# One change to an attention and recurrence kernel: first loads and products in another order, the image's values in a column group per head, the last projection begun on half its input with two steps held for it, and the last store on SyncE

## The chip, the cores and the metric

The kernel runs on one core of one Trainium2 chip. The metric is the device time of one execution in microseconds (us). The engines are TensorE (PE; its weight loads are PEld), VectorE (DVE), ScalarE (ACT), GpSimd (POOL) and SyncE (SP), which here only issues DMA transfers.

## The reference

Two layers with residual connections follow each other, all in float32:

```
q, k, v = split(x @ c_attn_w + c_attn_b)          # x: 8 x 512 x 512; 16 heads of 32
k = concat([cond @ uk_w.T + uk_b, k])             # one image key per sequence
v = concat([cond @ uv_w.T + uv_b, v])             # one image value per sequence
scores = where(key <= query + 1, q k' / sqrt(32), -10000) + [0, mask]
x = x + (softmax(scores) @ v) @ c_proj_w + c_proj_b
xw = x @ Wx + b                                   # for all 512 steps
h_t = tanh(h_{t-1} @ Wh + xw_t)                   # h_0 = cond
out = x + h
```

## The kernel before, in words

The 8 sequences of 512 positions are cut into 8 parts of 64 positions and two sets of four sequences: 16 trips (`TRIPS`), each of 4 sequences by 64 positions. A trip has 32 units (`UNITS`): a unit `u` is one head for two of its sequences. For each trip TensorE makes `q` and `k` in four chunks (`q`, `k`, `imgscore` for the image key), `v` in two halves (`vfirst`, `v`), for each unit `score`, `turn` (probabilities transposed), for every four units `pv`, for every 16 units `imgturn`, `rowturn` and `norm` (the image's part added to `pv`), and at the end the output projection `proj` in four chunks. Matrices that need accuracy are split into a high and a low part and multiplied in three products (lines 502 to 504). Keys and values go through DRAM (`k_dram`, `v_dram`): a store from POOL or SyncE, then loads by SyncE into `kt` and `vbuf`.

The recurrence has 512 steps. A step is 16 matmuls that each write one 32-row column group (line 1056), a transpose on DVE (line 882) and a tanh on ScalarE (line 735). 448 steps (`FIRST`) are laid between the attention work of trips 2 to 15, the last 64 follow behind the last projection. Each group of 16 steps (`out`) is transposed on TensorE, copied on ScalarE to `outs` (line 725) and stored by POOL (line 640).

What sets the order is the list that `main_order()` writes out: a pass over all units with a side list of dense work (projections of the next trip), and events without cost such as loads. `order()` places the steps in it (the `while` loop) and gives each engine its own list, sorted by the clock of TensorE's work plus a lag for each kind (`LAGS`). Every engine works its list strictly in order.

Ahead of the lists each engine has a fixed prologue. SyncE loads `ident`, `cond`, `uk_w`, four of the eight pieces of `w_qkv`, the `x` of trip 0, the other four pieces, `uv_w` and `w_proj`. TensorE transposes `cond` and `uk_w` (line 901), multiplies them (line 906, for the image key `kimg`), transposes `uv_w` (line 912, into the four `scores` banks, which ScalarE copies to `wh`, line 662), and begins with `q` of chunk 0. The product for the image value (`vimg`, line 946) comes behind chunk 0. ScalarE casts the pieces of `w_qkv` to their high part (line 651), four before and four after it casts the `x` of trip 0; DVE makes the low parts (lines 746 and 766). `wx` and `wh` hold these early matrices until POOL loads `w_x` and `w_h` into them (line 622). `wproj` on ScalarE and DVE (lines 697, 792) splits `w_proj`. ScalarE's `xsplit` (line 676) casts the `x` of the next trip, loaded by SyncE in `load_x` (line 527).

`norm` on TensorE is line 1021: for each of the four chunks one matmul of 32 rows (two sequences' 16 image probabilities) by 128 columns, into all 128 rows of `pv`. DVE then scales (`x1T`, line 860), ScalarE casts it (`attnT_hi`, line 715), DVE makes `attnT_lo` in two halves (line 865), each counted in `attn_split`; `proj` waits for all of them before its first matmul.

## Time and profile before

| | |
|---|---|
| median of 3 runs | 1640.55 us (1639.9 to 1641.07) |
| the profiled execution | 1643.75 us, of which the profile's span is 1642.0 us |
| TensorE busy | 1532.6 us (93%), 32749 matmul passes |
| DVE, ScalarE, POOL busy | 778.3, 665.1, 186.5 us |
| mean granted TensorE clock | 0.987 of full speed |
| chain that ended last | PE 86%, DVE 4%, issue 4%, ACT 4% |

### The profile page before, as it was taken

To read this page: it belongs to the slowest core of one execution; us is meant where nothing else is said; L and a number is where in the kernel's file an instruction comes from. 1 tells how busy PE (TensorE), PEld (TensorE's weight loads), DVE (VectorE), ACT (ScalarE), POOL (GpSimd) and SP (SyncE) were. 2 spreads that over 40 slices of the span, in tenths; PEclk is the share of its full clock that TensorE was granted. 3 is DMA by queue.
4 is the path that set the end of the run, shared out by engine and by line. 5 is a ranking of instruction groups with operands and counts; after the bars stand their busy time and mean duration, and the time that the engine had idled before them with its cause. 6 is when DMAs were issued, how large, how long until landed. Compare 5 with 4: busy or idle time off the path is not lost.

```text
span 1642.0 us, 74143 instructions
## 1 busy us (share of the span) xinstructions
PE 1532.6 (93%) x32749; PEld 1225.9 (75%) x32749; DVE 778.3 (47%) x2687; ACT 665.1 (41%) x2257; POOL 186.5 (11%) x300
## 2 busy tenths in 40 slices
PE   7799999999999999999999999999999999998775
PEld 6677887877777787877878778687787677777554
DVE  4455454445454545545455454554554454554221
ACT  3444444344343434344443443444534444443111
POOL 2111111010110101001010110100101011100000
PEclk9889999999999999999999999999999999999999
DMA  7323122212222223223332232333332332331000
GB/s 231 107 63 82 50 69 66 69 52 71 65 73 75 79 67 92 74 72 88 85 91 77 81 97 75 109 84 84 107 92 72 110 98 82 116 100 28 16 10 15
DMA packets 167903, 130.24 MB, mean 79 GB/s; under 512 B 54264, under 2 KB 153112, under 8 KB 167072
## 3 DMA queue, kind: packets, MB, share of 16 engines
q1 hardware_dynamic: 153792, 92.92, 19.9%
q0 software_dynamic: 13792, 32.58, 7.3%
q8 instruction: 260, 4.26, 1.1%
q14 instruction: 59, 0.48, 0.1%
HBM read 100.00 MB, written 25.43 MB: 76 GB/s over the span
## 4 chain that ended last, share of the span: by engine, by line
PE 86%; DVE 4%; issue 4%; ACT 4%; SPq 1%; DMA 1%; POOL 0%; DVEq 0%; POOLq 0%
PE rec L1056 27%; PE dense L986 10%; PE dense L502 9%; PE dense L504 7%; PE dense L503 7%; PE rec L1047 7%; PE scores L978 5%; PE pv L1003 4%; PE pv L1021 2%; PE scores L1056 2%; DVE pre L882 1%; PE dense L1063 1%; ACT probs L686 1%; ACT states L735 1%; PE dense L1014 1%
## 5 line engine op out<-in xcount | busy, mean ns | idle before, releaser
L1056 PE MATMUL rec<-wh,states 128*32 128x128 f32 x15360 | 516.3, 275 | 19.9 <-ACT states L735 19.2
L1056 PEld LDWEIGHTS rec<-wh,states 128*32 128x32 f32 x15360 | 399.3, 110 | 107.3 <-ACT states L735 46.1
L882 DVE STREAM_TRANSPOSE pre<-rec 128x128 f32<-128x128 f32 x480 | 152.0, 317 | 502.6 <-PE rec L1056 501.2
L735 ACT ACTIVATE states<-pre 128x32 f32<-128x32 f32 x512 | 133.9, 262 | 508.6 <-DVE pre L882 507.6
L686 ACT ACTIVATE probs<-probs,nmax 128x64 f32<-128x64 f32 (+7 forms) x512 | 271.3, 532 | 104.9 <-DVE nmax L826 102.5
L826 DVE CUSTOM_DVE_ANT_0 probs<-scores,msk,nimg 128x64 f32<-128x64 f32 (+7 forms) x512 | 245.2, 502 | 14.6 <-PE scores L978 6.4
L986 PE MATMUL dense<-ident,probs 128*128 128x128 f32 (+1 forms) x1254 | 229.2, 288 | 19.0 <-DVE probsT L836 7.0
L986 PEld LDWEIGHTS dense<-ident,probs 128*128 128x128 f32 (+1 forms) x1254 | 129.2, 135 | 82.1 <-issue 56.7
L502 PE MATMUL dense<-xT_hi,wqkv_hi 128*128 128x256 f32 x488 | 149.6, 307 | 6.7 <-DVE nimg L812 3.5
L836 DVE COPY probsT<-dense 128x256 f32<-128x256 f32 (+4 forms) x240 | 120.2, 501 | 63.3 <-PE dense L986 57.9
L694 ACT COPY probsT<-dense 128x256 f32<-128x256 f32 (+4 forms) x246 | 104.3, 424 | 107.0 <-PE dense L986 106.5
L1047 PE MATMUL rec<-wx,x 128*32 128x128 f32 x3840 | 133.8, 275 | 4.6 <-ACT rec L669 3.9
L504 PE MATMUL dense<-xT_hi,wqkv_lo 128*128 128x256 f32 x488 | 137.7, 282 | 0.0
L503 PE MATMUL dense<-xT_lo,wqkv_hi 128*128 128x256 f32 x488 | 137.5, 282 | 0.0
L1047 PEld LDWEIGHTS rec<-wx,x 128*32 128x32 f32 x3840 | 98.9, 109 | 27.7 <-issue 10.3
L508 POOL DMA_DIRECT2D k_dram<-knew x60 | 47.7, 795 | 612.0 <-DVE knew L802 584.3
L1003 PE MATMUL pv<-probsT,vbuf 128*32 128x64 f32 (+1 forms) x5120 | 103.8, 221 | 7.8 <-DMA vbuf<-v_dram 6.9
L502 PEld LDWEIGHTS dense<-xT_hi,wqkv_hi 128*128 128x128 f32 x488 | 92.6, 190 | 22.2 <-issue 10.2
L1003 PEld LDWEIGHTS pv<-probsT,vbuf 128*32 128x32 f32 (+1 forms) x5120 | 84.8, 109 | 25.1 <-issue 18.4
L978 PE MATMUL scores<-kt,q 32*64 32x64 f32 (+7 forms) x2048 | 97.3, 428 | 5.3 <-issue 4.8
L686 ACT ACTIVATION_READ_ACCUMULATOR probs<-probs,nmax 128x1 f32 x512 | 96.7, 189 | 0.0
L503 PEld LDWEIGHTS dense<-xT_lo,wqkv_hi 128*128 128x128 f32 x488 | 92.6, 190 | 0.2 <-issue 0.2
(138 smaller groups left out, 1766.3 us busy)
## 6 DMA issues: line engine op xcount, KB each, us to landing
vbuf<-v_dram SPq DMA_DIRECT2D x64, 192.0 KB, 2.7
xin<-x SPq DMA_DIRECT2D x64, 128.0 KB, 2.6
v_dram<-vbuf POOLq DMA_DIRECT2D x64, 128.0 KB, 2.8
out<-outs POOLq DMA_DIRECT2D x32, 256.0 KB, 4.2
vbuf<-v_dram SPq DMA_DIRECT2D x64, 128.0 KB, 2.4
kt<-k_dram SPq DMA_DIRECT2D x16, 512.0 KB, 5.6
vbuf<-v_dram SPq DMA_DIRECT2D x32, 256.0 KB, 3.2
k_dram<-knew POOLq DMA_DIRECT2D x60, 128.0 KB, 2.7
```

What stands on the lines that cost most here:

```text
L502: pe.matmul(out, hi, moving_hi, start=first, stop=False)
L503: pe.matmul(out, hi, moving_lo, start=False, stop=False)
L504: return pe.matmul(out, lo, moving_hi, start=False, stop=last)
L686: act.activation(probs[:, g % PROBS, 0:n], probs[:, g % PROBS, 0:n], ACT.Exp, scale=-1.0, bias=nmax[:, e, h:h + 1], accum_out=rowsum[:, e, ...
L735: act.activation(state_cells(g), pre[:].rearrange("p f (b z) -> p f b z", z=GROUP)[:, :, :, s], ACT.Tanh).then_inc(h_ready, 1)
L826: dve.tensor_tensor_reduce(out=probs[:, g % PROBS, 0:n], in0=scores[g % HC][:, 0:n], in1=msk[:, e, 0:n], scale=-SCALE, scalar=nimg[:, trip ...
L882: dve.transpose(pre_all, rec_bank(g // GROUP)[:, 0:P]).then_inc(pre_ready, 1)
L978: last = pe.matmul(scores[g % HC][W * b:W * b + W, 0:n], q[rows, trip % 2, c, at:at + W], heads_tile(group)[rows, b, :], start=True, stop= ...
L986: last = pe.transpose(bank(kind, g, 0)[0:min(P, n - at), at:at + P], probs[:, g % PROBS, at:min(at + P, n)], ident[:])
L1003: last = pe.matmul(pv[Q * j:Q * j + Q, P * c + W * b:P * c + W * b + W], vtile[g % VTILES][rows, b, at // P, Q * j:Q * j + Q], probsT[rows ...
L1047: pe.matmul(rec_bank(g)[Q * j:Q * j + Q, 0:P], x1_group(g)[:, f], wx[:, f, :].rearrange("p (a j c) -> p a j c", a=C, j=C)[:, :, j, :], sta ...
L1056: last = pe.matmul(rec_bank(g // GROUP)[Q * j:Q * j + Q, 0:P], state_tile(g - 1)[:, f, :], wh[:, f, P * j:P * j + P], start=False, stop=f ...
```

## The change

1. The beginning. `uk_w` is loaded in two halves of its columns, and TensorE begins each pair of transposes when its half is there. The product for the image key swaps its operands: the image state stands in a column group as in a step (16 matmuls of 32 columns), and DVE transposes the result before it fills `kimg`. `uv_w` is loaded ahead of the second four pieces of `w_qkv`, and its transposes become a kind of their own, `uvturn`, behind `q` and `k` of chunk 0. The `x` loads of trips 1 and 2 move from the end of chunk 2 to units 3 and 14, the loads of `w_proj` to unit 12 and its splits from units 5 to 8 to units 24 to 27, the loads of `w_x` and `w_h` from behind `vimg` to unit 20.
2. `norm` becomes 16 matmuls of 32 rows by 32 columns, one per head.
3. The last two of the 448 steps are held until just before the last projection, and the first chunk of every projection waits for `attn_split` in two parts.
4. The last `out` store is issued by SyncE and has a semaphore of its own.

```diff
@@ main_order
     emit([("mskload", 0, 0, 0.0), ("mskload", 0, 1, 0.0), ("mskscale", 0, 0, 0.0), ("mskscale", 0, 1, 0.0)]
-         + chunk(0, 0) + [("vimg", 0, 0, 3.7)] + chunk(0, 1) + chunk(0, 2) + [("xload", 1, 0, 0.0), ("xload", 2, 0, 0.0)])
+         + chunk(0, 0)[0:2] + [("uvturn", 0, 0, 3.6)] + chunk(0, 0)[2:] + [("vimg", 0, 0, 3.7)] + chunk(0, 1) + chunk(0, 2))
...
-        if g == 0 and h in (5, 6, 7, 8):
-            emit([("wproj", 0, h - 5, 0.0)])
+        if u == 3:
+            emit([("xload", 1, 0, 0.0)])
+        if u == 12:
+            emit([("wpload", 0, 0, 0.0)])
+        if u == 14:
+            emit([("xload", 2, 0, 0.0)])
+        if u == 20:
+            emit([("weights", 0, 0, 0.0)])
+        if g == 0 and h in (24, 25, 26, 27):
+            emit([("wproj", 0, h - 24, 0.0)])
@@ order
         while (t < FIRST and at > ends[(t // W + 1) * QUADS - 1]
+               and (t < FIRST - 2 or at + 1 == last)
                and (done >= max(whole * (t + 0.5) / FIRST, step_at + PACE) or at + 1 == last)):
...
+            if kind == "out" and name == ("POOL" if g == OUTS - 1 else "SP"):
+
+                continue
@@ sync
-            for tile, a in ((ident[:], ident_in), (cond_sb, cond), (uk_raw, uk_w)):
+            for tile, a in ((ident[:], ident_in), (cond_sb, cond)):
                 sp.dma_start(tile, a).then_inc(key_loaded, 16)
+            for k in range(2):
+                half = slice(D // 2 * k, D // 2 * (k + 1))
+                sp.dma_start(uk_raw[:, :, half], uk_w[:, :, half]).then_inc(uk_loaded[k], 16)
             for n, i in enumerate(SPLITS):
                 if n == C:
                     load_x(sp, 0)
+                    sp.dma_start(uv_raw, uv_w).then_inc(value_loaded, 16)
...
-            sp.dma_start(uv_raw, uv_w).then_inc(value_loaded, 16)
-            for c in range(C):
-                sp.dma_start(raw_proj[c], w_proj[:, c, :]).then_inc(proj_loaded, 16)
...
+                if kind == "wpload":
+
+                    sp.wait_ge(low_ready, 2 * C)
+                    for c in range(C):
+                        sp.dma_start(raw_proj[c], w_proj[:, c, :]).then_inc(proj_loaded, 16)
+                elif kind == "xload":
+                    if g == 1:
+
+                        sp.wait_ge(low_ready, C)
...
+                elif kind == "out":
+                    wait_copied(sp, kind, g, 0)
+                    sp.dma_start(out[:, g * HALF:(g + 1) * HALF, :], outs[:]).then_inc(last_stored, 16)
@@ gpsimd
+                elif kind == "weights":
+
+                    pool.wait_ge(setup_product, 2)
                     for tile, w in ((wx, w_x), (wh, w_h)):
                         pool.dma_start(tile[:], w).then_inc(weights_loaded, 16)
@@ scalar
-            for f, d in enumerate(scores):
-                act.wait_ge(setup_turned, C + 2 + f)
-                act.copy(wh[:, f, :], d[:, :]).then_inc(values_copied, 1)
...
+                elif kind == "uvturn":
+                    for f, d in enumerate(scores):
+                        act.wait_ge(setup_turned, C + 2 + f)
+                        act.copy(wh[:, f, :], d[:, :]).then_inc(values_copied, 1)
@@ vector
+            dve.transpose(pre_all, rec[:, 0:P]).then_inc(image_turned, 1)
+            dve.wait_ge(image_turned, 1)
@@ tensor
-            for c in range(C):
-                for f in range(C):
-                    last = pe.matmul(rec[:, B * c:B * c + B], wx[:, f, P * c:P * c + P], imgT[:, f, :],
-                                     start=f == 0, stop=f == C - 1)
+
+            pe.wait_ge(h_ready, 1)
+            for f in range(C):
+                for j in range(C):
+                    last = pe.matmul(rec[Q * j:Q * j + Q, 0:P], state_tile(-1)[:, f, :],
+                                     wx[:, f, :].rearrange("p (a j c) -> p a j c", a=C, j=C)[:, :, j, :],
+                                     start=f == 0, stop=f == C - 1, skip_group_check=True)
...
                     for c in range(C):
-                        last = pe.matmul(pv[:, P * c:P * c + P], vimg[:, P * c:P * c + P], pimgT[:],
-                                         start=False, stop=True, skip_group_check=True)
+                        for j in range(HC):
+
+                            at = P * c + Q * j
+                            last = pe.matmul(pv[Q * j:Q * j + Q, P * c:P * c + P], vimg[:, at:at + Q], pimgT[:],
+                                             start=False, stop=True, skip_group_check=True)
...
-                    if i == 0:
-                        pe.wait_ge(attn_split, 4 * g + 4)
                     for c in range(C):
+                        if i == 0 and c % 2 == 0:
+
+                            pe.wait_ge(attn_split, 4 * g + 3 + c // 2)
```

The order of the engines' instructions shows the moves. TensorE at the start of the program, before (`imgT` is the image state, `vbuf` holds `uv_w`, `spread` the image state broadcast for `vimg`; rows of one kind are left out after the first three):

```order
L901 MATMUL scores<-ident,probsT 128x128 x16
L906 MATMUL rec<-imgT,wx 128x8 x16
L912 MATMUL scores<-ident,vbuf 128x128 x16
L502 MATMUL dense<-xT_hi,wqkv_hi 128x256
L503 MATMUL dense<-xT_lo,wqkv_hi 128x256
L504 MATMUL dense<-xT_hi,wqkv_lo 128x256
```

And in the changed kernel, with the end of chunk 0:

```order
L938 MATMUL scores<-ident,probsT 128x128 x16
L945 MATMUL rec<-wx,states 32x128 x16
L518 MATMUL dense<-xT_hi,wqkv_hi 128x256
L519 MATMUL dense<-xT_lo,wqkv_hi 128x256
L520 MATMUL dense<-xT_hi,wqkv_lo 128x256
L981 MATMUL scores<-ident,vbuf 128x128 x16
L998 MATMUL rec<-kimg,q 64x4 x4
L987 MATMUL scores<-wh,spread 128x512 x4
```

The 16 transposes of `uv_w` moved from ahead of all 24 matmuls of `q` and `k` to behind them, directly ahead of the image score and of `vimg`.

SyncE's queue around the first `v` loads, before (`kt` and `vbuf` loads of keys and values, `xin` loads of `x`, `k_dram` stores of keys):

```order
L508 DMA k_dram<-knew 128x4x64
L578 DMA kt<-k_dram 128x2x64
L527 DMA xin<-x 128x4x64 x8
L508 DMA k_dram<-knew 128x4x64
L578 DMA kt<-k_dram 128x2x64
L595 DMA vbuf<-v_dram 64x128 x4
L578 DMA kt<-k_dram 128x2x64 x2
L595 DMA vbuf<-v_dram 64x128 x2
```

And in the changed kernel:

```order
L524 DMA k_dram<-knew 128x4x64
L603 DMA kt<-k_dram 128x2x64
L623 DMA vbuf<-v_dram 64x128 x4
L543 DMA xin<-x 128x4x64 x4
L603 DMA kt<-k_dram 128x2x64 x2
L577 DMA x<-w_proj 128x512 x4
L623 DMA vbuf<-v_dram 64x128 x2
```

The eight `x` loads stood ahead of the last `k` store and the `v` loads; now four stand behind the `v` loads, the other four and `w_proj` later.

TensorE ahead of the last projection, before (`pimg` and `spread` are transposed for `norm`):

```order
L1010 MATMUL dense<-ident,pimg 32x128
L1014 MATMUL dense<-ident,spread 128x128 x4
L1056 MATMUL rec<-wh,states 32x128 x16
L1003 MATMUL pv<-probsT,vbuf 32x64 x32
L1021 MATMUL pv<-pimgT,vimg 128x128 x4
L1056 MATMUL rec<-wh,states 32x128 x16
L502 MATMUL dense<-attnT_hi,wproj_hi 128x256
```

And in the changed kernel:

```order
L1051 MATMUL dense<-ident,pimg 32x128
L1055 MATMUL dense<-ident,spread 128x128 x4
L1044 MATMUL pv<-probsT,vbuf 32x64 x32
L1065 MATMUL pv<-pimgT,vimg 32x128 x16
L1101 MATMUL rec<-wh,states 32x128 x32
L518 MATMUL dense<-attnT_hi,wproj_hi 128x256
```

One step moved from ahead of `pv` to behind `norm`, so that two steps follow one another there; `norm` has 16 matmuls where it had 4.

## Rows read from the trace of the kernel before

**Rows 1.** The page, part 1: busy us, share of the span, instructions.

```profile
PE 1532.6 (93%) x32749; PEld 1225.9 (75%) x32749; DVE 778.3 (47%) x2687; ACT 665.1 (41%) x2257; POOL 186.5 (11%) x300
```

**Rows 2.** Table by stage: length, then busy time by engine, clock, DMA share, GB/s.

```profile
400.00:1300.00 900.00, 873.33 (x19208) 694.04 (x19201) 445.96 (x1469) 379.80 (x1246) 105.86 (x161) 1.00 0.30 84
1580.00:1600.00 20.00, 14.38 (x455) 11.42 (x448) 4.66 (x14) 3.35 (x14) 0.60 (x1) 1.00 0.07 16
```

**Rows 3.** Timeline of the beginning: start us, us, engine, line, operation, idle before.

```profile
15.67 1.28 DVE L766 TENSOR_TENSOR xT_lo<-xin,xT_hi 128x512 fp32r<-128x512 f32 x2
...
20.16 0.83 ACT L651 CAST wqkv_hi<-vbuf 128x768 fp32r<-128x768 f32 x1 [0.17 <-DMA vbuf<-w_qkv]
...
23.25 3.58 PE L912 MATMUL scores<-ident,vbuf 128*128 128x128 f32 x16 [4.25 <-DMA vbuf<-uv_w]
...
26.87 0.59 ACT L662 COPY wh<-scores 128x512 f32<-128x512 f32 x1 [0.17 <-PE scores L912]
...
28.36 0.48 ACT L679 ACTIVATE q<-dense,bqk 128x256 f32<-128x256 f32 x1 [0.91 <-PE dense L504]
...
29.94 3.70 PE L946 MATMUL scores<-wh,spread 128*128 128x512 f32 x8
...
33.07 0.68 PE L502 MATMUL dense<-xT_hi,wqkv_hi 128*128 128x256 f32 x1
```

**Rows 4.** Chain of waits around one `norm`: start us, us, what.

```profile
916.66 0.87 PE rec L1056 x32
...
923.13 1.08 PE pv L1021 x8
924.21 1.01 PE rec L1056 x32
```

**Rows 5.** Table by stretches, columns as in rows 2: the clock is third last.

```profile
54.00:55.00 1.00, 0.00 (x0) 0.00 (x0) 0.96 (x4) 0.59 (x3) 0.00 (x0) 0.50 1.12 286
...
67.00:68.00 1.00, 1.00 (x9) 1.00 (x8) 0.00 (x0) 0.16 (x2) 0.00 (x0) 0.72 0.20 56
...
1505.00:1511.00 6.00, 5.79 (x27) 5.82 (x28) 1.21 (x7) 0.00 (x0) 0.00 (x0) 0.50 0.00 0
1512.00:1514.00 2.00, 1.91 (x16) 1.70 (x15) 0.91 (x5) 0.00 (x0) 0.00 (x0) 1.00 0.04 8
```

**Rows 6.** Timeline, 47 to 73 us.

```profile
47.59 5.04 SPq L527 DMA_DIRECT2D xin<-x  x8
47.86 1.09 POOL L636 DMA_DIRECT2D v_dram<-vbuf  x2 [10.75 <-DVE vbuf L808]
...
53.11 1.14 ACT L676 CAST xT_hi<-xin 128x512 fp32r<-128x512 f32 x2
...
59.83 0.65 PE L1003 MATMUL pv<-probsT,vbuf 64*32 64x64 f32 x16 [6.92 <-DMA vbuf<-v_dram]
...
72.58 0.43 PE L1003 MATMUL pv<-probsT,vbuf 64*32 64x64 f32 x16
```

**Rows 7.** Timeline at the last projection and, the last two rows, two late steps.

```profile
1500.94 1.15 PE L1021 MATMUL pv<-pimgT,vimg 32*128 32x128 f32 x8
...
1504.31 0.75 DVE L865 TENSOR_TENSOR attnT_lo<-x1T,attnT_hi 128x256 fp32r<-128x256 f32 x2
...
1505.21 0.55 PE L502 MATMUL dense<-attnT_hi,wproj_hi 128*128 128x256 f32 x1 [2.10 <-DVE attnT_lo L865]
...
1599.07 1.08 PE L1056 MATMUL rec<-wh,states 128*32 128x128 f32 x32 [0.51 <-ACT states L735]
...
1600.88 1.08 PE L1056 MATMUL rec<-wh,states 128*32 128x128 f32 x32 [0.51 <-ACT states L735]
```

**Rows 8.** DMA issues: count, KB of each, median us from issue to landing.

```profile
xin<-x SPq DMA_DIRECT2D x64, 128.0 KB, 2.6
v_dram<-vbuf POOLq DMA_DIRECT2D x64, 128.0 KB, 2.8
out<-outs POOLq DMA_DIRECT2D x32, 256.0 KB, 4.2
```

More of the change, by code:

```diff
@@ L403, in attention_recurrence @@
         image_ready = sem("image_ready")
+        image_turned = sem("image_turned")
+        uk_loaded = [sem(f"uk_loaded{k}") for k in range(2)]
         kimg_ready = sem("kimg_ready")
@@ L899, in _ @@
             for f, d in enumerate(scores):
+                if f % 2 == 0:
+                    pe.wait_ge(uk_loaded[f // 2], 16)
                 for o in range(C):
@@ L941, in _ @@
                         last.then_inc(dense_ready, 1)
+                elif kind == "uvturn":
+                    pe.wait_ge(value_loaded, 16)
+                    for f, d in enumerate(scores):
+                        for o in range(C):
+                            last = pe.transpose(d[:, P * o:P * o + P], uv_raw[:, o, P * f:P * f + P], ident[:])
+                        last.then_inc(setup_turned, 1)
                 elif kind == "vimg":
```

21 lines of the change are left out of this document (9 added, 12 removed).

## The prediction

> **What bounds the kernel now.** I read the page first: TensorE is busy for 93% of the span [rows 1]. So time is won only where TensorE gets less to do, works faster or waits less. The table by stage [rows 2] says where. From 400 to 1300 us it is busy 873 of 900 us, at the full clock: there only less work helps. From 1580 to 1600 us it is busy 14.4 of 20: the last recurrence steps follow one another, each waiting for the last, and whatever precedes them shifts them whole. For the beginning and the last projection I read the timeline [rows 3, 6, 7], for the `norm` matmuls the chain of waits [rows 4], for TensorE's clock the table by stretches [rows 5], for the last store the DMA issues [rows 8].
>
> **The beginning up to chunk 1.** Before, the first `q` matmuls of chunk 0 stand behind the 16 `uv_w` transposes (line 912), which wait for their load until 23.25 us and take 3.58 us [rows 3]. The operands of `q` are there far earlier: the two DVE instructions that make `xT_lo` begin at 15.67 us and take 1.28 us together [rows 3]. After the change `q` and `k` of chunk 0 can run from 16.4 us. The product of line 906 becomes 16 narrow matmuls like a step, about 1 us [rows 4]; nothing waits on that saving, since `xT_lo` comes later.
> The gain does not pass through whole. ScalarE must cast the last four pieces of `w_qkv` before it copies `q`. The last of these casts starts at 20.16 us [rows 3]; now `uv_w` is loaded ahead of those pieces. In the trace `uv_w` lands 23.25 - 20.16 = 3.1 us after the last piece, so I move the last piece by that: cast from 23.25 to 24.1, `q` copied (0.48) at 24.6, then four copies of `uv` at 0.59 each, until 27.0 [rows 3]. Only then can the `vimg` product start, which takes 33.07 - 29.94 = 3.1 us [rows 3]. Chunk 1 then starts at 30.1 instead of 33.07, 2.9 us earlier.
> But TensorE will have stood nearly idle for some 2 us ahead of `vimg`. The trace shows the clock at 0.50 (1.2 GHz) after such stretches, at 54 and at 1505 us, and back at 1.00 (2.4 GHz) only after work from 59.83 to about 67.6 and from 1505.21 to some time after 1511 [rows 5, 6, 7]. I charge 4.2 us of work at the low level, where it takes twice its time, so 2.1 us. **0.8 us remains**; the ends are 2.9 (no fall) and -1.0 (7.8 us at the low level).
> The 24 matmuls of `q` and `k` may run at the low level too: 27 projection matmuls of this shape took 5.79 us [rows 5], 0.214 each, so 5.1 us, to 21.5; the transposes (3.58) end at 25.1. ScalarE's 27.0 covers this; without that cover it would cost the whole difference to the full level, up to 2.3 us.
> `uk_w` in two halves lets the first transposes begin earlier, which nothing waits for. Its rows shrink from 8 to 1 KB. The nearest row is `uv_w`, 1 MB in 3.1 us; I bound the cost by 0 and a third of that, 1 us, and take 0, as the trace shows nothing for a loss. The Trainium skill (DMA: Bandwidth & Descriptors, Bandwidth) says to batch transfers into at least 1 MiB to reach 75% of peak. By it the split costs something, and the sum would be smaller by up to 1 us (estimate).
>
> **The beginning, 45 to 62 us.** SyncE issues the eight `x` loads of trips 1 and 2 from 47.59 us for 5.04 us; the store of `k` chunk 3 and the `v` loads stand behind them, and TensorE waits 6.92 us for a `v` tile, until 59.83 [rows 6]. After the change `x` and `w_proj` stand behind the `v` loads. The two `v` stores go out from 47.86, the second at 48.4, and land in 2.8 us [rows 6, 8], so the loads are issued from 51.2 at about 0.6 us each, and the first pair lands near 54.5: `pv` 5.3 us sooner.
> What is late next is on ScalarE. The cast of `x` for trip 1 (two, 1.14 us at 53.11) [rows 6] stands ahead of the softmax that the third turn behind that `pv` needs. The four `x` loads of trip 1 are issued from 53.6 to 56.1 (half of 5.04), the last lands 2.6 us after its start [rows 8], at 58.1; one cast (0.57) and the softmax (0.5) follow. That turn moves from about 60.8 to 59.2: **1.6 us**. Bounds: 5.3 (the `x` is in time) and 0.
> `w_proj` (1 MB) now stands ahead of the loads of `v` group 2, `w_x` and `w_h` (2 MB) between two `k` stores on POOL. I cost both at nothing. The `pv` of group 2 runs at 72.58 [rows 6], its load can be issued once the first `pv` is done, over 10 us before, and 1 MB takes 3.1 us. Without this cover each would cost up to its own loading time, 3 and 6 us. The casts of `w_proj` on ScalarE and DVE come later, where both are about half busy [rows 2]. The share of low clock in later stretches I leave as it is. Beginning: 0.8 + 1.6 = **2.4 us**.
>
> **`norm`, 32 times.** Each has 8 passes of 32 rows by 128 columns, 1.08 us in the chain [rows 4]. A step, 32 passes of 32 columns for the same number of columns in all, takes 0.87 us in one place and 1.01 in another, where transposes of the full width follow [rows 4]. The new form has 32 rows, its neighbours 128. Bounds: 0.07 and 0.21 us each, 2.2 and 6.7 in all. I take 0.14, the middle, and nine tenths of it, since TensorE is 97% busy there [rows 2]: **4.0 us**. The step's 1.01 against its 0.87 is 0.14 us where the form changes. The Trainium skill (TensorEngine Tiling (Array Packing), Key Properties) says that a change of tiling mode drains the engine, and the rows agree. By it the new form, with a change on either side, would take the 1.01, and `norm` would bring 2.2.
>
> **The last projection.** Before, a step lies ahead of the last `pv`, and after the last `norm` (from 1500.94) another; then TensorE waits 2.10 us for `attnT_lo`, until 1505.21 [rows 7]. Now `pv` and `norm` come a step (about 1.0) sooner and both steps follow. `norm` ends near 1501.0; the steps start at 1501.0 and 1502.8 (1600.88 - 1599.07 = 1.81 apart [rows 7]), the second ends near 1503.7. `attnT_lo` was ready 3.0 us after the end of `norm` (1502.0), with a step's work on DVE ahead of its two parts of 0.38 [rows 7]; now it stands ahead of that work, and its first half is enough: 1503.3 at the latest. So the projection starts at 1503.75, **1.4 us** sooner, and the wait on half the input is covered by the steps and worth nothing.
> The clock fell in that idle time: 27 matmuls in 5.79 us, later 16 in 1.91 [rows 5], 0.214 and 0.119 each; over some 29 of them 2.8 us were lost. With 0.8 us as the longest idle piece (the last steps, a quarter idle, hold 1.00 [rows 2]) I expect it kept and take 0.85 of it, **2.4 us**. Bounds of the whole place: 1.0 and 4.3.
>
> **The last store.** POOL's `out` stores land after 4.2 us; a load of half the size by SyncE lands in 2.6, a store of half the size by POOL in 2.8 [rows 8]. Bounds 0 (the landing is the store's own) and 1.6; I take the middle, **0.8 us**. The Trainium skill (DMA: Bandwidth & Descriptors, Latency and other measured facts) puts the first byte at about 0.6 us for SyncE's kind and 1 us for POOL's: by it 0.4 us (estimate).
>
> **Sum.** 2.4 + 4.0 + 3.8 + 0.8 = 11.0 us. The profiled execution took 1643.75 us, and would take 1632.75; the median of the runs, 1640.55, is 3.2 us lower, so 1629.5.
>
> **The rivals.**
> *The clock falls at the last projection all the same.* The second step still waits 0.8 us, and TensorE waits before 1499 us too. 2.4 us are not won: 1631.9. Chance 0.14.
> *The beginning keeps its clock.* If neither `vimg` nor the work behind the `v` wait meets the low level, 2.1 and half of 7.8 us more are won: 1623.5. For it: the long wait shrinks. Against: some of it stays. Chance 0.14.
> *The beginning gives nothing*, because ScalarE stands longer at the `x` of trip 1 and low stretches grow: 2.4 won becomes 2 lost, 1633.9. Chance 0.12.
> *The narrow `norm` passes do not overlap, and the kernel is slower.* Place: the 32 `norm` groups. If the 32 passes ran one after another at today's 0.135 us, a group would take 4.3 us, 103 us more in all, and the kernel 1736. It decides from 41 ns a pass on: the other places bring 7.0 us, 0.22 per group, and (1.08 + 0.22)/32 = 0.041. A step's passes take 27 to 32 ns [rows 4]. Against: 16 `pv` passes on 64 rows, also a part of the height, take 0.43 us [rows 6]. Chance 0.04.
> *Nothing that can be measured:* small losses in all places keep it within 0.2% (3.3 us, about what a measurement of this kernel can tell from no change). Chance 0.04.
>
> **How the numbers follow.** The forecast has 0.52, with a range of its own from 1625 to 1633. The neighbouring rivals widen it to 1621 to 1635, which leaves out the last two and the tails, below 0.2. Faster by over 0.2% is below 1637.3: 0.52 + 0.14 + 0.14 and most of 0.12, 0.90; same 0.05, slower 0.05.
>
> **What would show it.** The first `q` near 16.4 us; chunk 1 near 30; the wait for a `v` tile down to 1 or 2 us, with a new wait for a softmax behind it; each `norm` at 0.87 to 1.01 us in the chain; the projection directly behind the steps, the clock at 1.00 in it; a last store that lands sooner. I am wrong if a `norm` still takes 1.08, if 0.50 stands in the last projection, or if chunk 1 starts after 32.

## The result and the profile after

The changed kernel takes **1633.16 us** (median of 11 runs, 1631.52 to 1637.88) beside 1641.07 us for the kernel before in the same comparison (11 runs, 1639.9 to 1646.42). The ratio is 0.9944, with a 95% interval from 0.9933 to 0.9955: faster by 0.56%, 9.2 us by the ratio and 7.9 by the two medians. The forecast was 1629.5 us with a range from 1621 to 1635. A second comparison gave 1633.69 beside 1641.99 us, ratio 0.995 [0.9931, 0.9969].

| | before | after |
|---|---|---|
| the profiled execution | 1643.75 us | 1632.09 us |
| its span | 1642.0 us | 1630.1 us |
| mean granted TensorE clock | 0.987 | 0.992 |
| chain that ended last | PE 86%, DVE 4%, issue 4%, ACT 4% | PE 86%, DVE 5%, ACT 4%, issue 3% |

The two profiled executions differ by 11.7 us, more than the medians do, because the one of before lay 2.7 us above its median and the other 1.1 us below. Single executions of the kernel before went from 1637.5 to 1649.4 us over the comparisons. So a place is compared below not only with the profiled before but also with the experiments that leave that place as it was.

The page's part 1 of the changed kernel (busy us, share of the span, instructions):

```profile
PE 1521.4 (93%) x33517; PEld 1211.5 (74%) x33517; DVE 779.0 (48%) x2688; ACT 665.0 (41%) x2257; POOL 188.3 (12%) x299
```

Against [rows 1], TensorE is busy for 11.2 us less, with 768 passes more: 32 `norm` groups of 32 passes in place of 8. The other engines' busy times are within 2 us of what they were, and the 93% too.

The table by stage answers to [rows 2] (length, busy time of PE, PEld, DVE, ACT, POOL, clock, DMA share, GB/s):

```profile
400.00:1300.00 900.00, 873.24 (x19648) 691.78 (x19641) 447.47 (x1468) 382.77 (x1251) 105.74 (x161) 1.00 0.30 84
```

The middle is as full as it was; the same 900 us only get a little further in the work.

**The beginning.** The timeline of the changed kernel up to chunk 1 (start us, us, engine, line, operation, idle before):

```profile
9.76 1.97 PE L938 MATMUL scores<-ident,probsT 128*128 128x128 f32 x8 [1.86 <-DMA probsT<-uk_w]
10.69 0.83 ACT L683 CAST wqkv_hi<-x 128x768 fp32r<-128x768 f32 x1 [8.68 <-DMA x<-w_qkv]
...
18.09 0.55 PE L518 MATMUL dense<-xT_hi,wqkv_hi 128*128 128x256 f32 x1 [3.64 <-DVE xT_lo L799]
...
23.35 1.91 PE L981 MATMUL scores<-ident,vbuf 128*128 128x128 f32 x16
...
24.55 0.83 ACT L683 CAST wqkv_hi<-vbuf 128x768 fp32r<-128x768 f32 x1 [0.19 <-DMA vbuf<-w_qkv]
25.29 0.47 ACT L712 ACTIVATE q<-dense,bqk 128x256 f32<-128x256 f32 x1
25.66 2.04 ACT L709 COPY wh<-scores 128x512 f32<-128x512 f32 x4
27.75 3.70 PE L987 MATMUL scores<-wh,spread 128*128 128x512 f32 x8 [1.45 <-ACT wh L709]
30.89 0.68 PE L518 MATMUL dense<-xT_hi,wqkv_hi 128*128 128x256 f32 x1
```

The second half of `uk_w` is transposed from 9.76 us, and the first cast of `w_qkv` waits until 10.69 (7.97 before). The first `q` comes 8.5 us sooner than before (26.58), but `vimg` only 2.2 us: as predicted ScalarE's casts decide. The last cast, from 20.16 [rows 3] to 24.55 us, is even later than the 23.25 I had taken. Against that, `vimg` ran at the full clock here and took 3.14 us. Chunk 1 begins 2.2 us sooner. The 24 matmuls of `q` and `k`, from 18.09 to 23.35 us, did run at the low level, as the prediction allowed for: they stand 0.21 us apart (0.12 at the full one), although the clock column reads 1.00 there. So in this first stretch the spacing of the matmuls has to be read and not the column.

The same view from 48 to 58 us, with SyncE's DMA issues (SPq):

```profile
48.77 2.43 SPq L623 DMA_DIRECT2D vbuf<-v_dram  x4
...
51.25 2.24 SPq L543 DMA_DIRECT2D xin<-x  x4
...
52.78 0.65 PE L1044 MATMUL pv<-probsT,vbuf 64*32 64x64 f32 x16 [2.04 <-DMA vbuf<-v_dram]
...
54.35 0.62 ACT L705 CAST xT_hi<-xin 128x512 fp32r<-128x512 f32 x1 [3.31 <-DMA xin<-x]
...
55.89 0.62 ACT L705 CAST xT_hi<-xin 128x512 fp32r<-128x512 f32 x1 [0.93 <-DMA xin<-x]
...
56.91 0.42 PE L1027 MATMUL dense<-ident,probs 128*64 128x128 f32 x1 [2.91 <-ACT probs L719]
```

TensorE's wait for a `v` tile went from 6.92 [rows 6] to 2.04 us, and behind it stands the new one: 2.91 us for a softmax, which ScalarE reaches only after the two casts of `x` for trip 1, which wait for their loads. What was late next is what the prediction named.

**`norm`.** The chain of waits around one `norm` (start us, us, what):

```profile
914.65 1.01 PE pv L1065 x32
915.66 1.01 PE rec L1101 x32
```

A group fell from 1.08 [rows 4] to 1.01 us, and the step behind it stayed at 1.01. In the chain 31 of the 32 groups stand at 1.08 before (the other at 2.00) and all 32 at 1.00 to 1.05 in the changed kernel.

**The last projection and the last store.** The timeline of TensorE and DVE at the projection:

```profile
1492.39 1.08 PE L1065 MATMUL pv<-pimgT,vimg 32*32 32x128 f32 x32
1493.40 1.08 PE L1101 MATMUL rec<-wh,states 128*32 128x128 f32 x32
1493.54 0.75 DVE L895 TENSOR_TENSOR x1T<-pv,spread 128x256 f32<-128x256 f32 x2 [2.88 <-PE pv L1065]
1494.43 0.76 DVE L900 TENSOR_TENSOR attnT_lo<-x1T,attnT_hi 128x256 fp32r<-128x256 f32 x2
1495.11 0.31 DVE L917 STREAM_TRANSPOSE pre<-rec 128x128 f32<-128x128 f32 x1
1495.77 1.08 PE L1101 MATMUL rec<-wh,states 128*32 128x128 f32 x32 [1.29 <-ACT states L768]
1496.78 0.39 PE L518 MATMUL dense<-attnT_hi,wproj_hi 128*128 128x256 f32 x1
...
1503.79 1.08 PE L1092 MATMUL scores<-wx,x 128*32 128x128 f32 x32 [1.00 <-issue]
```

And the table by stretches at the projection (columns as in the table above, clock third last):

```profile
1496.00:1502.00 6.00, 6.00 (x75) 5.80 (x68) 3.04 (x14) 0.63 (x3) 0.00 (x0) 1.00 0.00 0
```

The projection follows the second step without a wait, and the clock is 1.00 where [rows 5] had 0.50: its matmuls stand 0.12 us apart, not 0.214. From its first matmul to the next `xW` part it takes 7.01 us, before 9.69. The two steps, however, start 2.37 us apart, not 1.81: DVE works through `x1T` and both parts of `attnT_lo` before it turns to the first step's transpose.

The end of the program:

```profile
1621.72 0.59 ACT L758 COPY outs<-dense 128x512 f32<-128x512 f32 x1 [1.22 <-PE dense L1108]
1622.33 0.71 SPq L607 DMA_DIRECT2D out<-outs  x1
```

From the end of the copy (1622.31) to the end of the span (1630.1) it is 7.79 us, before 8.57. SyncE begins to issue 0.02 us after the copy; POOL, in the kernel before, began 0.28 us after its end at 1633.43:

```profile
1633.71 0.60 POOL L640 DMA_DIRECT2D out<-outs  x1 [24.00 <-ACT outs L725]
```

### The profile page after: what moved, and what is told of

Read it like the earlier page. It is cut to its first block, busy times and chain, and to the rows that moved or that the text cites. A ratio compares the mean times of both kernels' runs of the same rounds, so it can differ in the third digit from the quotient of the medians.

```text
span 1630.1 us, 75682 instructions
## 1 busy us (share of the span) xinstructions
PE 1521.4 (93%) x33517; PEld 1211.5 (74%) x33517; DVE 779.0 (48%) x2688; ACT 665.0 (41%) x2257; POOL 188.3 (12%) x299
## 4 chain that ended last, share of the span: by engine, by line
PE 86%; DVE 5%; ACT 4%; issue 3%; SPq 1%; DMA 1%; DVEq 0%; POOL 0%; ACTq 0%
PE rec L1101 28%; PE dense L1027 10%; PE dense L518 9%; PE rec L1092 7%; PE dense L520 7%; PE dense L519 7%; PE scores L1019 5%; PE pv L1044 4%; PE scores L1101 2%; PE pv L1065 2%; DVE pre L917 1%; ACT states L768 1%; PE dense L1108 1%; ACT probs L719 1%; PE dense L1055 1%
## 5 line engine op out<-in xcount | busy, mean ns | idle before, releaser
L719 ACT ACTIVATE probs<-probs,nmax 128x64 f32<-128x64 f32 (+7 forms) x512 | 271.3, 531 | 105.0 <-DVE nmax L861 102.2
L1044 PE MATMUL pv<-probsT,vbuf 128*32 128x64 f32 (+1 forms) x5120 | 103.9, 221 | 2.2 <-DMA vbuf<-v_dram 2.0
```

The costliest lines, as they stand in the source:

```text
L719: act.activation(probs[:, g % PROBS, 0:n], probs[:, g % PROBS, 0:n], ACT.Exp, scale=-1.0, bias=nmax[:, e, h:h + 1], accum_out=rowsum[:, e, ...
L1044: last = pe.matmul(pv[Q * j:Q * j + Q, P * c + W * b:P * c + W * b + W], vtile[g % VTILES][rows, b, at // P, Q * j:Q * j + Q], probsT[rows ...
```

## The experiments

The same marks were read from the profile of every run: the start of `vimg` and of chunk 1; the first `pv`; the first write of the first trip's projection (some 102 us); at the end, the last `rowturn` transposes, the last projection, the next `xW` part, and the time from the last `outs` copy to the end of the span. Single executions differ in where the clock is low, so a mark of one run is good to a few us in the beginning, and to some 0.1 us over a short piece at full clock.

### Each part alone on the kernel before

Four kernels each add one of the change's four parts to the kernel before; 12 runs each, beside 35 of the kernel before (median 1641.72 us). `begin_only` has part 1, all of it, whose core is:

```diff
-         + chunk(0, 0) + [("vimg", 0, 0, 3.7)] + chunk(0, 1) + chunk(0, 2) + [("xload", 1, 0, 0.0), ("xload", 2, 0, 0.0)])
+         + chunk(0, 0)[0:2] + [("uvturn", 0, 0, 3.6)] + chunk(0, 0)[2:] + [("vimg", 0, 0, 3.7)] + chunk(0, 1) + chunk(0, 2))
```

> The kernel before with the beginning of the change alone. Theory (the parts add up): the profile of the changed kernel is ahead by 6.7 us when the first projection's results are written, of which part is clock luck, so 4 to 7 us faster than before. Rival (what was predicted): 2.4 us faster. Rival (the gain at the beginning is eaten later by the recurrence): within 1 us of before.

`norm_only` has part 2:

```diff
-                        last = pe.matmul(pv[:, P * c:P * c + P], vimg[:, P * c:P * c + P], pimgT[:],
+                        for j in range(HC):
+                            at = P * c + Q * j
+                            last = pe.matmul(pv[Q * j:Q * j + Q, P * c:P * c + P], vimg[:, at:at + Q], pimgT[:],
```

> The kernel before with the 16 narrow matmuls of norm alone. Theory (a form of 32 rows changes the form towards the step behind it, and the group takes 1.01 us instead of 1.08): 32 x 0.07, 1 to 2.5 us faster, 1.01 in the chain. Rival (as predicted): 4 us faster, 0.87 to 0.94 in the chain.

`tail_only` has part 3:

```diff
+               and (t < FIRST - 2 or at + 1 == last)
...
-                        pe.wait_ge(attn_split, 4 * g + 4)
+                            pe.wait_ge(attn_split, 4 * g + 3 + c // 2)
```

> The kernel before with the two held steps and the half-input wait alone. Theory: the projection starts 0.7 us sooner and runs at the full clock; faster by 0.7 us plus the 2.7 us of the low clock wherever the kernel before meets it, so 1 to 3.5 us in the median. Rival (the clock in the kernel before is low there only in the profiled execution): 0.7 us.

`store_only` has part 4:

```diff
+                elif kind == "out":
+                    wait_copied(sp, kind, g, 0)
+                    sp.dma_start(out[:, g * HALF:(g + 1) * HALF, :], outs[:]).then_inc(last_stored, 16)
```

> The kernel before with the last out store on SyncE alone. Theory: the end of the copy to the end of the span shrinks from 8.57 us by 0.8, all of it in the time. Rival (the end is set by something else, such as the barrier behind the stores): no change within 0.3 us.

| kernel | median us | ratio to before [95%] |
|---|---|---|
| begin_only | 1639.29 | 0.9985 [0.997, 1.0] |
| norm_only | 1639.83 | 0.9981 [0.9966, 0.9996] |
| tail_only | 1640.85 | 0.9988 [0.9973, 1.0003] |
| store_only | 1642.29 | 1.0003 [0.9991, 1.0015] |

The four ratios add up to 0.43% (0.15 + 0.19 + 0.12 - 0.03), the whole change gave 0.56 and 0.50%. Each ratio is uncertain by about 0.15%, so this is compatible with parts that add, and does not prove it. Only the interval of `norm_only` excludes no change; `begin_only` is at the edge, the other two can't be told from nothing. `begin_only` gave 2.4 us where its theory had 4 to 7: its rival, the 2.4 of the prediction, held. The sizes are better read from the traces.

*Beginning.* The first `pv` of the four runs with the old beginning stood at 59.83, 60.36, 60.38 and 60.53 us; in those with the new one, as the change wrote it, at 51.7 to 54.7. These 7 us are mostly given back by 102 us: the first write of the projection stood at 108.16, 102.16, 106.01 and 103.62 with the old beginning (mean 105.0) and at 103.9, 101.41, 102.98, 102.18, 101.85 and 103.01 with the new (mean 102.6). **2.4 us** are kept, with an uncertainty of over 1 us, since the old beginning alone varies by 6 us.

*`norm`.* In the chain of `norm_only` all 32 groups take 1.00 or 1.01 us, as in the changed kernel, and the steps behind them 1.01 (one 1.05): its theory. The 2.2 us that this makes are too few to be seen in the long stretch from the first write of the second trip's projection to the last `rowturn`, which took 1275.7 to 1278.2 us in the four profiles with the old `norm` and 1279.5 in `norm_only`.

*Last projection.* From the last `rowturn` transposes to the next `xW` part the four runs without the held steps took 16.42, 15.21, 15.12 and 15.20 us, `tail_only` 13.02 and the changed kernel 12.99. Only the first of the four profiles lost as much as the prediction had counted: it took 9.69 us from the projection to the `xW` part, the other three 8.46 to 8.47, `tail_only` 7.00. So the held steps bring 0.7 us by an earlier projection and 1.5 us by the clock; 2.7 only against the first profile.

*Last store.* From the copy to the end, like with like: with the old beginning 8.57, 8.49 and 8.46 us where POOL stores and 8.17 where SyncE does (`store_only`); with the new beginning 8.15 where POOL stores (`begin_only`) and 7.79 to 7.87 in the eight where SyncE does (mean 7.84). So the store by SyncE is worth **0.3 us**, of which 0.26 is the earlier start of its issue (the end of the span is known to 0.1 us). Another 0.35 us comes with the new beginning, whoever stores; why is not shown. No median could show either.

### Is the `norm` group at 1.01 because of its form?

`norm_rows128` keeps the changed kernel's 32 passes of 32 columns, but gives them the 128 rows of their neighbours: `vimg` and `pimgT` have 96 more rows of zeros, so the sum is the same.

```diff
-        vimg = sb("vimg", [2 * H, D])
+        vimg = sb("vimg", [P, D])
...
-        pimgT = sb("pimgT", [2 * H, P])
+        pimgT = sb("pimgT", [P, P])
...
+            for r in range(1, HC):
+                dve.memset(vimg[Q * r:Q * r + Q, :], 0.0).then_inc(zeroed, 1)
+                dve.memset(pimgT[Q * r:Q * r + Q, :], 0.0).then_inc(zeroed, 1)
```

> The changed kernel with norm on all 128 rows (rows 32 to 127 of vimg and of pimgT are zeros), so that its 16 matmuls have the form of a step. Theory (a change of form towards the step behind it makes the group 1.01 us): the group takes 0.87 us in the chain, 32 x 0.14 = 4.5 us less, and from the second write of projection results to the last rowturn 4 us less than in the changed kernel (1275.1 us, of which 1.5 by the clock). Rival (32 rows are slower in themselves): also 0.87. Rival (1.01 is the price of any group of this size there): 1.01, no change.

1628.1 us (4 runs), ratio 0.9916 [0.9902, 0.9929]: 0.3% faster than the changed kernel, about 5 us by the ratios to before (the two were not run side by side). Its chain around the same `norm`:

```profile
913.20 1.01 PE pv L1070 x32
914.21 0.87 PE rec L1106 x32
```

Here the group itself did not get shorter; the step **behind** it fell from 1.01 to 0.87 us. Ahead of this group stand transposes of full width, another form. The next `norm` in the chain stands behind a step, and there the group itself fell. `norm_rows128`:

```profile
955.29 1.01 PE rec L1106 x32
956.30 0.87 PE pv L1070 x32
```

and the changed kernel:

```profile
956.63 1.01 PE rec L1101 x32
957.64 1.01 PE pv L1065 x32
```

So a group of 32 such passes takes 1.01 us behind a group of another form and 0.87 behind one of its own, whichever of the two is the `norm`. Over all 32 places the chain of `norm_rows128` has 15 groups behind a step (or the `xW` part, which has the same form) at 0.87 or 0.88, one behind `pv` at 0.92, and the 16 behind transposes and other work at 1.01 (one of them at 1.79). A step follows eleven of those 16, and now takes 0.87; a step follows seven of the first 15, and takes 0.94 or 0.95 instead of 1.01 (why not 0.87 is not shown). That is 15 + 11 times 0.14, 7 times 0.07 and 0.1 once: 4.2 us, most of the gain in the median. The stretch from the second trip's projection to the last `rowturn` took 1268.8 us, and 1274.1 to 1277.8 in the six other profiles of the changed kernel and its variants with a `norm` of 32 rows; the expectation had 4 us less. The theory was right that the form is the cause, but named the wrong neighbour: what counts is the group ahead. So the group itself reached its 0.87 in half of the places. That 32 rows are slower in themselves is ruled out by the places behind transposes, where both forms take 1.01. The kernel before shows the same: its step at 0.87 [rows 4] has ahead of it a group of its own form (the `xW` part, line 1047), which itself stands behind transposes:

```profile
915.65 1.01 PE rec L1047 x32
```

### What does the split of `uk_w` cost?

`uk_whole` is the changed kernel with `uk_w` in one transfer.

```diff
-            for k in range(2):
-                half = slice(D // 2 * k, D // 2 * (k + 1))
-                sp.dma_start(uk_raw[:, :, half], uk_w[:, :, half]).then_inc(uk_loaded[k], 16)
+            sp.dma_start(uk_raw, uk_w).then_inc(uk_loaded[0], 16)
```

> The changed kernel with uk_w loaded by one DMA, as before. Theory (the halves with 1 KB rows load slower and delay everything behind them): the first piece of w_qkv is cast near 8.0 us instead of 10.69, the first q starts near 16.5 instead of 18.09, the last cast starts near 23.3 instead of 24.55 and chunk 1 near 29.6 instead of 30.89. Rival (uv_w ahead of x or the queue order delays them): all as in the changed kernel.

1630.91 us (5 runs), ratio 0.9934 [0.9921, 0.9946]; the interval overlaps that of the changed kernel, so the time leans to a gain and does not prove it. Its timeline does show the cost. SyncE's queue at the start, `uk_whole`:

```profile
1.59 0.36 SPq L561 DMA_DIRECT2D probsT<-uk_w  x1
1.99 0.90 SPq L567 DMA_DIRECT2D x<-w_qkv  x2
```

and the changed kernel:

```profile
1.61 1.35 SPq L563 DMA_DIRECT2D probsT<-uk_w  x2
3.00 1.11 SPq L569 DMA_DIRECT2D x<-w_qkv  x2
```

The rows further on, `uk_whole`:

```profile
8.30 0.83 ACT L681 CAST wqkv_hi<-x 128x768 fp32r<-128x768 f32 x1 [6.29 <-DMA x<-w_qkv]
...
22.93 0.83 ACT L681 CAST wqkv_hi<-vbuf 128x768 fp32r<-128x768 f32 x1 [0.36 <-DMA vbuf<-w_qkv]
...
26.13 5.40 PE L985 MATMUL scores<-wh,spread 128*128 128x512 f32 x8 [1.44 <-ACT wh L707]
30.96 0.69 PE L518 MATMUL dense<-xT_hi,wqkv_hi 128*128 128x256 f32 x1
```

The first cast of `w_qkv` comes at 8.30 us instead of 10.69, the last at 22.93 instead of 24.55, `vimg` at 26.13 instead of 27.75. Over all profiles the first cast stands at 7.97 to 8.68 us in the six with `uk_w` whole (mean 8.4) and at 9.60 to 10.69 in the seven with halves (mean 10.1); the last cast, with the new order of loads, at 22.93 and 23.67 with `uk_w` whole (`combo` is the other) and at 23.63 to 24.80 with halves (mean 24.5). **The split costs 1.7 us at the first load behind it and 1.2 us at the last**, 1.6 in this pair of profiles. Of the 1.7 us, 1.0 is there already when SyncE issues the first piece of `w_qkv`: the two halves take it 1.35 us to issue, the whole 0.36. Besides, SyncE's queue moved 1.44 MB in the first 8 us, against 1.79 MB in `uk_whole`, in 1290 packets against 533. Whether the shorter rows or the second transfer make the difference was not separated. But here `vimg` met the low clock, and took 4.83 us where the changed kernel's profile has 3.14. The table by stretches shows it, `uk_whole`:

```profile
26.00:31.00 5.00, 4.87 (x9) 2.10 (x9) 0.00 (x0) 0.07 (x1) 0.00 (x0) 0.66 0.24 52
```

and the changed kernel:

```profile
26.00:31.00 5.00, 3.56 (x17) 1.79 (x17) 0.84 (x3) 1.70 (x4) 0.93 (x2) 1.00 0.19 41
```

So chunk 1 started at 30.96 us, as in the changed kernel (30.89), and not at the expected 29.6. The low clock in `vimg` is not the doing of this edit alone: of the six profiles with the beginning as the change wrote it, three have `vimg` at 3.14 us (`begin_only`, the changed kernel, `norm_rows128`) and three at 4.84, among them `again`, which is the same kernel. None of the four with the old beginning has it. What differs shows in the work ahead of it. The changed kernel's transposes of `uv_w` start at 23.35 us, since its `q` and `k` stayed at the low level to the end; in `again` the last seven of them ran 0.12 us apart, and the transposes started 0.8 us sooner:

```profile
22.53 1.91 PE L981 MATMUL scores<-ident,vbuf 128*128 128x128 f32 x16
...
27.84 5.40 PE L987 MATMUL scores<-wh,spread 128*128 128x512 f32 x8 [1.44 <-ACT wh L709]
```

Behind them TensorE has only the image score (0.40 us) until ScalarE is ready for `vimg`. So the sooner the clock rose, the longer it stood idle, and the clock fell. The same holds for all nine profiles with this order: from the first of these transposes to `vimg` it is 4.4 to 4.8 us in the three at the full clock and 5.0 to 5.8 in the six at the low one, with `uk_whole` at 5.0. No experiment changed this idle time on purpose, so that it is the cause is argued from these profiles and not tested; nor is it shown that `uk_w` in one piece would keep its 1.6 us, since both profiles that have it with the new order met the low clock.

### The softmax behind the loads of `x`

`x_early` issues the loads of `x` for trip 1 at the end of chunk 2 again, those of trip 2 stay late.

```diff
-         + chunk(0, 0)[0:2] + [("uvturn", 0, 0, 3.6)] + chunk(0, 0)[2:] + [("vimg", 0, 0, 3.7)] + chunk(0, 1) + chunk(0, 2))
+         + chunk(0, 0)[0:2] + [("uvturn", 0, 0, 3.6)] + chunk(0, 0)[2:] + [("vimg", 0, 0, 3.7)] + chunk(0, 1) + chunk(0, 2) + [("xload", 1, 0, 0.0)])
...
-        if u == 3:
-            emit([("xload", 1, 0, 0.0)])
```

> The changed kernel with the x loads of trip 1 back at the end of chunk 2 (those of trip 2 stay at unit 14). Theory (ScalarE waits 3.3 and 0.9 us for them, and TensorE 2.91 us for the softmax behind): that wait of TensorE is gone, the turn behind it comes near 54 instead of 56.91 us, the first pv stays near 52.8; the results of the first projection come 3 us or more sooner. Rival (the store of k chunk 3 is delayed and the v loads with it): pv 1 us or more later and no gain.

1630.47 us (5 runs), ratio 0.9928 [0.9915, 0.9942]. In its timeline ScalarE's casts wait for nothing, and the transposes of softmaxes follow the first `pv`:

```profile
52.72 1.14 ACT L703 CAST xT_hi<-xin 128x512 fp32r<-128x512 f32 x2
...
54.51 0.43 PE L1042 MATMUL pv<-probsT,vbuf 64*32 64x64 f32 x16 [2.00 <-DMA vbuf<-v_dram]
...
55.01 0.60 PE L1025 MATMUL dense<-ident,probs 128*64 128x128 f32 x2
```

The wait of 2.91 us is gone; for a softmax TensorE waits 0.5 us in all between 30 and 110 us. The wait for the `v` tile did not grow. (All of it stands 1.7 us late, since `vimg` ran at the low clock in this profile too.) So the part of the change that moved the `x` of trip 1 behind the `v` loads made the new wait. But the expectation had the results of the first projection 3 us sooner, and that did not come: their first write stands at 102.42 us, against 101.85 to 103.01 in the three without this edit (`again`, `step_first`, `full_wait`) whose `vimg` met the low clock as well. The table by stretches shows where the lead went, `x_early`:

```profile
90.00:102.00 12.00, 11.48 (x111) 8.04 (x110) 3.94 (x20) 4.47 (x22) 1.82 (x4) 0.61 0.19 46
```

and `again`:

```profile
90.00:102.00 12.00, 10.71 (x161) 7.34 (x162) 6.98 (x40) 6.69 (x34) 2.98 (x7) 0.86 0.21 54
```

The clock was lower there, by a quarter of 12 us. The profile is that of the slowest of the five executions (1636.03 us), and whether the others kept the lead is not shown. By the ratios to before the gain is about 3 us, and the interval overlaps that of the changed kernel, as with `uk_whole`.

### The order of DVE at the last projection, and the wait on half the input

`step_first` lets DVE transpose the first held step ahead of the two parts of `attnT_lo`:

```diff
+                late = 0.3 if (name, kind, g) == ("DVE", "attnlow", 2 * TRIPS - 1) else 0.0
+                plan[name].append((clock + lags.get(kind, 0.0) + late, kind, g, i))
```

> The changed kernel with the transpose of the first held step ahead of attnT_lo on DVE. Theory (the step's transpose stands behind attnT_lo, so the steps are 2.37 us apart instead of 1.81): steps 1.81 apart, rowturn to projection 5.4 us instead of 5.98. Rival (attnT_lo is then late): a wait for attnT_lo takes its place and the projection starts as before.

`full_wait` is the changed kernel with the wait of before, on the whole input, in every projection:

```diff
+                    if i == 0:
+                        pe.wait_ge(attn_split, 4 * g + 4)
...
-                            pe.wait_ge(attn_split, 4 * g + 3 + c // 2)
```

> The changed kernel with the first projection chunk waiting for all of attnT_lo again. Theory (the two steps cover the whole of attnT_lo): the last projection starts 5.98 us after the last rowturn, as in the changed kernel. Rival (the half-input wait is what brings it forward): 0.4 us or more later.

`step_first` took 1632.65 us (5 runs), ratio 0.9941 [0.9928, 0.9953], which can't be told from the changed kernel. Its timeline shows the two steps 1.82 us apart:

```profile
1494.69 1.08 PE L1102 MATMUL rec<-wh,states 128*32 128x128 f32 x32
1496.51 1.08 PE L1102 MATMUL rec<-wh,states 128*32 128x128 f32 x32 [0.73 <-ACT states L769]
1497.52 0.39 PE L519 MATMUL dense<-attnT_hi,wproj_hi 128*128 128x256 f32 x1
```

From `rowturn` to the projection it takes 5.42 us instead of 5.98, and the projection still waits for nothing, though its input is now later. `full_wait` (one run, 1632.74 us, with the kernel before at 1641.99) has 5.98 us there, like the changed kernel, and its projection too waits for nothing behind the step:

```profile
1497.37 0.39 PE L518 MATMUL dense<-attnT_hi,wproj_hi 128*128 128x256 f32 x1
```

The wait on half the input is worth nothing at this place, by this one profile.

### The findings together, and the changed kernel once more

`combo` has the edits of `norm_rows128`, `uk_whole`, `x_early` and `step_first` together; `again` is the changed kernel as it is.

```diff
-         + chunk(0, 0)[0:2] + [("uvturn", 0, 0, 3.6)] + chunk(0, 0)[2:] + [("vimg", 0, 0, 3.7)] + chunk(0, 1) + chunk(0, 2))
+         + chunk(0, 0)[0:2] + [("uvturn", 0, 0, 3.6)] + chunk(0, 0)[2:] + [("vimg", 0, 0, 3.7)] + chunk(0, 1) + chunk(0, 2) + [("xload", 1, 0, 0.0)])
...
-        vimg = sb("vimg", [2 * H, D])
+        vimg = sb("vimg", [P, D])
```

> The changed kernel with norm on 128 rows, uk_w loaded whole, the x of trip 1 early and the step's transpose ahead of attnT_lo. Theory (the four effects lie in different places and add): 4.5 + 1.6 + about 2 + 0.6 us, of which the clock may give back some; 1624 to 1627 us, ratio to before 0.989 to 0.991. Rival (the low clock fills what the waits leave): no better than norm_rows128 alone, 0.9916.

> The changed kernel itself, once more, beside combo. Theory (the spread between executions is where the clock happens to fall, and the places of the change add up to 7 to 9 us): ratio to before 0.994 to 0.996 and, in the profile, about 13.0 us from the last rowturn to the next part of xW, at the full clock. Rival (the first measurement was lucky): above 0.996.

`combo` took **1623.69 us** (4 runs, 1621.67 to 1624.46), ratio 0.9887 [0.9869, 0.9906], with the changed kernel at 1633.69 (6 runs, 1630.89 to 1637.19) on the same chip. It beats both kernels: 1.1% under the one before, 10 us under the changed one in the same comparison, slightly better than its theory (1624 to 1627 us). Singly the four edits lowered the ratio from 0.9947 (the middle of the two comparisons) by 0.31, 0.13, 0.19 and 0.06%, together 0.69%; `combo` is 0.6% lower. In its profile the gain stands at the places of the edits: the first write of the first projection comes at 98.92 us (102.6 in the mean of the six with the beginning as the change wrote it), the stretch from the second projection to the last `rowturn` takes 1271.1 us (1275.4 in the mean of the six with a `norm` of 32 rows), and from there to the next `xW` part it is 12.16 us (12.99). `again` came as expected: 0.995 and 12.98 us, at the full clock.

## Why the prediction was right, point by point

The sign was right, the time within the stated range, and each of the four places shows a gain in the traces; the sum of 11.0 us was 2 to 3 too high (9.2 and 8.2 us by the two ratios, 7.9 and 8.3 by the medians). The time of 1633.16 us lies 3.7 above the forecast, just outside the 1625 to 1633 that the forecast had of its own. Of this 3.1 us are the sum's excess over the 7.9 us of the medians; the rest is there because the median of before was 0.5 us higher in the longer comparison. By its steps:

- **Up to chunk 1**: predicted 0.8 us, a gain of 2.9 less a loss of 2.1 to the clock. Chunk 1 began at 33.07, 34.22, 33.70 and 34.19 us with the old beginning and at 30.55, 30.89, 29.96 and, with the low clock in `vimg`, 32.82, 32.68 and 32.64 with the new: 2.2 us in the mean. The clock does fall, but in three of the six profiles, and costs 1.7 us (4.84 - 3.14) there. In those three chunk 1 started after 32 us, which I had named as a sign of being wrong: there a low stretch met a last cast that came 1.4 us later than I had put it. So the 0.8 was too little in the mean, and single profiles have from 1.0 to 3.8 us. This is the rival that the beginning keeps its clock, true for half of them in `vimg` and for none behind the `v` wait: every profile has a piece of 4 us between 54 and 62 us with the clock at 0.50 to 0.52.
- **The split of `uk_w`**: I took 0 of my bounds 0 to 1, "as the trace shows nothing for a loss". It cost 1.2 us in the mean, 1.6 in the pair of profiles, beyond the bound. I had bounded it by the transfer itself; the cost lies with the loads queued behind it, whose first arrival moved by 1.7 us in the mean, 1.0 of it by the longer issue on SyncE, which the sum did not have at all. The rule of the Trainium skill (DMA: Bandwidth & Descriptors, Bandwidth) that speaks for transfers of 1 MiB and more had the sign right, and the trace agrees with it in that: first casts at 10.1 against 8.4 us in the mean.
- **45 to 62 us**: 1.6 us predicted. The mechanism was right to the piece (wait 6.92 to 2.04, then 2.91 us for the softmax behind the casts). In the profiled pair the third turn behind the first `pv` moved from about 60.8 to 56.91, 3.9 us, of which 2.2 came from chunk 1: 1.7 of its own. By 102 us the mean gain of the beginning is 2.4 us in all. That this is the predicted 2.4 is luck: it is made up of other pieces, over 1 us of what this turn had gained was lost again on the way, and the mean is uncertain by over 1 us.
- **`norm`**: predicted 4.0 us, measured about 2.2 (32 times 0.07 by the rows; 0.19%, with an interval from 0.04 to 0.34%, for `norm_only`). This is the mis-sized term. I took the middle between 0.87 and 1.01 us, though the new form of 32 rows differs from the neighbours on both sides; the case for 1.01 stood in the prediction and was right. I had also read [rows 4] the wrong way round, by what follows a step. The step at 0.87 is followed by matmuls of full width as well; what sets it apart is the group of its own form ahead of it. The Trainium skill (TensorEngine Tiling (Array Packing), Key Properties) says that a change of tiling mode drains the engine; by it the prediction gave 2.2. The trace agrees that a change of form costs something: 0.14 us, in the group that comes behind it (`norm_rows128`).
- **The last projection**: 3.8 us predicted, 3.4 measured against the first profile (16.42 to 12.99), 2.2 against the three others, where the low stretch was shorter; the 2.4 us for the clock were mis-sized by that, and measured 1.5. The clock did stay at 1.00. The projection came 0.75 us sooner, not 1.4: I set the steps 1.81 us apart and placed the `attnT_lo` work ahead of the step's transpose on DVE without charging the step for it. `step_first` gives 0.56 of the 0.65 back. That the half-input wait is worth nothing was right (`full_wait`, one run).
- **The last store**: 0.8 predicted, 0.3 measured, like with like; I took the middle of bounds read from other transfers. The Trainium skill's figures (DMA: Bandwidth & Descriptors, Latency and other measured facts) gave 0.4 as an estimate. The size fits, but the trace has 0.26 of the 0.3 before the issue begins, and shows nothing of a first byte.

Taken together the measured terms are 2.4 + 2.2 + 2.2 + 0.3 = 7.1 us, and 0.35 more at the end that nobody predicted, where the ratios say 9.2 (7.4 to 11.0) and 8.2 (5.1 to 11.3). What remains of 1 to 2 us is about the size of the intervals and of the scatter of the beginning, and stays open. That stretches of low clock later in the program differ as well was seen in single profiles and not traced further.

The rival that narrow passes don't overlap fell with the first row of the chain: 32 passes in 1.01 us are 32 ns each, below the 41 from which it would have decided. The rival of a clock that falls at the last projection fell too: 1.00 in every profile with the held steps.

## What to carry to other kernels

When a group of narrow matmuls stands between groups of another form, look at the group behind it as well: giving it the neighbours' form with rows of zeros cost no time and won about twice what the narrowing had (4.2 against 2.2 us by the rows). When a load is moved behind another, ask which engine works its list in order behind the consumer of that load; here moving the `x` of trip 1 made a wait of 2.91 us, which went when it was moved back, though the profile shows the lead lost again to the clock. Bound the cost of splitting a transfer by its issue and by the arrival of what is queued behind it, not by the transfer. And compare a place only between runs that are alike elsewhere: the last store seemed to bring 0.55 us over all profiles, and 0.3 like with like.

## What the hardware showed that I had not expected

- A change of form costs 0.14 us in the group that comes **behind** it. A `norm` of 128 rows took 0.87 us behind a step and 1.01 behind transposes; one of 32 rows took 1.01 behind either, and the step behind it 1.01 where it takes 0.87 behind a `norm` of 128 rows. Fewer rows with the same 32 columns count as another form.
- Two transfers with 1 KB rows in place of one with larger rows made the loads behind them later, by 1.7 us at the first and 1.2 us at the last (means over the profiles); SyncE took 1.35 us to issue the two and 0.36 for the one.
- The same kernel's `vimg` product took 3.14 us in one execution and 4.84 in another, though it began at 27.75 and 27.84 us. The work ahead of it had been done 0.8 us sooner in the second, because the clock had risen sooner, and the idle time before `vimg` was longer by as much. Such differences are some of the scatter between executions, and one profile of each kernel can show a gain some us larger or smaller than the medians do.
